# Routing, experts and combination of a top-2 mixture-of-experts layer in one block: two threshold bits a step, tokens gathered by slot, expert weights kept, last norm by tile

## The reference, cut to what matters

```
logits = xf @ router_w.T ; probs = softmax(logits)        # 2048 tokens, 8 experts
topw, topi = top_k(probs, 2) ; topw = topw / (topw.sum + 1e-6)
order = lexsort((-fw, fe))                                 # by expert, then by falling weight
rank = arange(N * K) - starts[se] ; keep = rank < capacity # capacity = 320
disp[e, slot] = xf[token]                                  # 8 x 320 rows of 128
eo = (silu(disp @ wg) * (disp @ wu)) @ wd                  # 128 -> 512 -> 128, by expert
out[token] += eo[expert, slot] * weight * keep
x = layernorm(x + out)
```

## Time and profile before

| | us |
|---|---|
| three timed runs | 2526.57, 2539.88, 2541.69 |
| median | 2539.88 |
| the profiled execution's own time | 2530.64 |
| its span, first to last instruction | 2528.8 |

### The profile page before, as it was taken

One profiled execution on the slowest core, in us unless ns is written; L12 is line 12 of the kernel. 1 busy time (PEld: TensorE's weight loads), 2 busy tenths in 40 slices (PEclk: granted clock), 3 DMA queues, 4 the chain that ended last, 5 costly groups with the idle time before them and its releaser, 6 DMA issues. The chain is left out here.

```text
span 2528.8 us, 55963 instructions
## 1 busy us (share of the span) xinstructions
PE 2023.5 (80%) x20339; PEld 1352.8 (53%) x20339; DVE 1867.9 (74%) x3645; ACT 1636.9 (65%) x3008; POOL 1248.1 (49%) x1115
## 2 busy tenths in 40 slices
PE   4388888279999999999999999999999998311370
PEld 2133332236776767777677767777677766210250
DVE  5566661389999999999999999999999993354013
ACT  2045556158888888888888888888888886100120
POOL 0100000177777677777777766777777762001415
PEclk8589998689999999999999999999999999555695
DMA  2412300311111120112101110112101110000222
GB/s 84 82 15 27 40 2 2 110 41 35 32 30 35 35 78 28 35 35 79 35 27 35 59 55 27 35 35 79 35 27 35 35 35 18 23 26 6 75 94 50
DMA packets 69952, 105.66 MB, mean 42 GB/s; under 512 B 21942, under 2 KB 44092, under 8 KB 69020
## 3 DMA queue, kind: packets, MB, share of 16 engines
q1 hardware_dynamic: 66996, 96.61, 14.1%
q0 software_dynamic: 2688, 5.51, 0.8%
HBM read 41.73 MB, written 10.42 MB: 21 GB/s over the span
## 5 line engine op out<-in xcount | busy, mean ns | idle before, releaser
L755 PE MATMUL pA<-layer_weights,x_feature_major 128*128 128x512 f32 x768 | 400.1, 603 | 32.4 <-DMA window_mask<-in_mask_dram 16.4
L1328 POOL TENSOR_TENSOR qk<-rot_cos,rot_sin 128x512 f32<-128x512 f32 x256 | 323.6, 1275 | 156.0 <-DVE rot_sin L1129 156.0
L1127 DVE TENSOR_TENSOR rot_cos<-pA,layer_tab 128x512 f32<-128x512 f32 x384 | 262.8, 684 | 76.7 <-ACT sq L968 70.3
L399 ACT ACTIVATE probs_by_key<-pT 128x512 f32<-128x512 f32 (+3 forms) x384 | 176.5, 489 | 206.9 <-PE pT L352 173.1
L1338 POOL TENSOR_TENSOR qk<-qk,rnorm 128x512 f32<-128x512 f32 x256 | 263.5, 1045 | 88.6 <-DVE rnorm L1162 88.6
L968 ACT ACTIVATE sq<-pA 128x512 f32<-128x512 f32 x384 | 228.5, 595 | 67.5 <-PE pA L755 58.0
L417 DVE TENSOR_REDUCE minus_max<-pS 128x1 f32<-128x1024 f32 (+7 forms) x256 | 184.2, 753 | 110.3 <-PE pS L326 110.0
L1139 DVE TENSOR_REDUCE sumsq<-sq 128x8 f32<-128x512 f32 x384 | 253.4, 671 | 14.6 <-ACT sq L968 14.4
L1129 DVE TENSOR_TENSOR rot_sin<-pA,layer_tab 128x512 f32<-128x512 f32 x384 | 260.8, 679 | 0.0
L1028 ACT ACTIVATE probsT<-pD 64x512 f32<-64x512 f32 x384 | 226.3, 589 | 43.7 <-PE pD L796 40.2
L1345 POOL TENSOR_TENSOR probs<-probs,row_inverse 128x1024 f32<-128x1024 f32 x96 | 182.7, 1903 | 101.6 <-DVE row_inverse L1198 101.6
(11 more groups left out here) (285 smaller groups left out, 4374.6 us busy)
## 6 DMA issues: line engine op xcount, KB each, us to landing
v_shifted<-v SPq DMA_DIRECT2D x96, 384.0 KB, 3.5
v_shifted<-v SPq DMA_DIRECT2D x95, 128.0 KB, 3.4
layer_weights<-in_Wqkv_dram SPq DMA_DIRECT2D x24, 384.0 KB
q_stack<-stacked SPq DMA_DIRECT2D x72, 64.0 KB
k_stack<-stacked SPq DMA_DIRECT2D x72, 64.0 KB
stacked<-part SPq DMA_DIRECT2D x24, 128.0 KB, 1.9
layer_weights<-in_Wo_dram SPq DMA_DIRECT2D x6, 512.0 KB
w_gate<-in_wg_dram SPq DMA_DIRECT2D x8, 256.0 KB, 2.7
```

Source lines behind the costliest of these rows:

```text
L755: pe.matmul(A[c % 2][:, :], cols(X0f, s), slot(s, QKV_AT + 512 * c, 512), start=True, stop=True).then_inc(q_ready[c], 1)
L1127: dve.tensor_tensor(t1[c % 2][:, :].rearrange("p (h g d) -> p h g d", g=2, d=32), a, tabl[s % 2][:, j].unsqueeze(1).broadcast_to([P, 8, 2, ...
L1328: pool.tensor_tensor(qk(s, c), t1[c % 2][:, :], t2[c % 2][:, :], ALU.add).then_inc(added[c], 1)
```

## The change

Lines with + are new and lines with - are removed. `route`, `experts`, `combine`, the last `layernorm_all` and `store_tokens` become one block, `routed_experts`. The tokens (x_stored) and all weights of all experts are sent from SP at its start.

The parts that change:

- The key is turned on TensorE, so that its 128 (tile, expert) pairs lie on the partitions and the 128 tokens of a tile on the free axis. The threshold takes 15 unrolled steps of two bits, three candidates each; the compare also writes its own count.
- Slots are counted along the free axis by a scan. The value goes back through TensorE to token order, and a product of two one-hot matrices (32 matmuls) gives the token of each slot (`idx`).
- GpSimd gathers the 20 slot tiles from DRAM into SBUF. No row is scattered or zeroed.
- Each gathered tile is turned once. TensorE's order is up(e, 0), down(e-1), up(e, 1 to 3), turn(e+1). Results are stored from SP, one buffer per expert.
- The norm's statistics are taken by tile behind the sums, the power by batches of 4, 4, 4, 2 and 2 tiles on GpSimd between its gathers, and the result is stored by batch.

```diff
+    TURNS = [(-(-e * CAP // P), -(-(e + 1) * CAP // P)) for e in range(EX)]
+    LN_BATCHES = [(0, 4), (4, 8), (8, 12), (12, 14), (14, 16)]
...
         @block.sync
+            sp.dma_start(w["tokens_in"].rearrange("(t p) d -> p t d", p=P), X[:, :, :]).then_inc(x_stored, 16)
+            for e in range(EX):
+                sp.dma_start(WG[:, e, :], w["wg"][e]).then_inc(w_loaded[e], 16)
+                sp.dma_start(WU[:, e, :], w["wu"][e]).then_inc(w_loaded[e], 16)
+                sp.dma_start(WD[:, e, :, :], w["wd"][e].rearrange("(c p) n -> p c n", p=P)).then_inc(w_loaded[e], 16)
+            for e in range(EX):
+                at = e * CAP
+                sp.wait_ge(y_kept, e + 1)
+                sp.dma_start(w["expert_out"][at:at + CAP - PARTIAL, :].rearrange("(c p) d -> p c d", p=P), yo[e][:, 0:CT - 1, :])\
+                    .then_inc(y_stored, 16)
+                sp.dma_start(w["expert_out"][at + CAP - PARTIAL:at + CAP, :], yo[e][0:PARTIAL, CT - 1, :]).then_inc(y_stored, 16)
+            out = w["result"].rearrange("(t p) d -> p t d", p=P)
+            for t0, t1 in LN_BATCHES:
+                sp.wait_ge(normed, t1)
+                sp.dma_start(out[:, t0:t1, :], X[:, t0:t1, :]).then_inc(stored, 16)
+            sp.wait_ge(stored, 16 * len(LN_BATCHES))
 
...
         @block.tensor
+            pe.wait_ge(key_done, 1)
+            pe.transpose(bank[0][:, 0:P], key[:, :, :].rearrange("p t e -> p (t e)"), ident[:, :]).then_inc(key_turned, 1)
+            for i in range(BIT_STEPS):
+                pe.wait_ge(compared, 3 * i + 3)
+                pe.matmul(bank[6][:, 0:3], cst[:, SUM_AT:SUM_AT + P], cnt[:, :], start=True, stop=True).then_inc(counted, 1)
+            pe.wait_ge(tile_counted, 2)
+            pe.matmul(bank[7][:, 0:2], cst[:, AHEAD_AT:AHEAD_AT + P], ncol[:, :], start=True, stop=True)
+            pe.matmul(bank[7][:, 2:3], cst[:, SUM_AT:SUM_AT + P], ncol[:, 0:1], start=True, stop=True).then_inc(offset_ready, 1)
+            pe.wait_ge(val_done, 2)
+            for k in range(2):
+                mm = pe.matmul(bank[0][:, 0:P], val[:, k, :], ident[:, :], start=(k == 0), stop=(k == 1))
+            mm.then_inc(val_ready, 1)
+            pe.wait_ge(eq_done, 2)
+            pe.wait_ge(ids_p, 1)
+            for c in range(PICKS):
+                if c % 8 == 0:
+                    pe.wait_ge(hot_done, c // 8 + 1)
+                mm = pe.matmul(bank[1][:, 0:2 * SLOT_TILES], hotL[:, c, :], hotR[:, c, :, :], start=(c == 0), stop=(c == PICKS - 1))
...
+            def turn(e):
+                t0, t1 = TURNS[e]
+                pe.wait_ge(slots_in[e], 16 * (t1 - t0))
+                if e >= 2:
+                    pe.wait_ge(xt_kept, e - 1)
+                for t in range(t0, t1):
+                    mm = pe.transpose(XT[e % 2][:, (t - t0) * P:(t - t0 + 1) * P], xg[:, t, :], ident[:, :])
+                mm.then_inc(xt_ready, 1)
...
+            turn(0)
+            for e in range(EX):
+                up(e, 0)
+                if e >= 1:
+                    down(e - 1)
+                for f in range(1, FC):
+                    up(e, f)
+                if e + 1 < EX:
+                    turn(e + 1)
+            down(EX - 1)
...
         @block.gpsimd
+            pool.wait_ge(x_stored, 16)
+            pool.wait_ge(idx_done, 1)
+            for e in range(EX):
+                for t in range(*TURNS[e]):
+                    pool.indirect_dma_start(out=xg[:, t, :], out_offset=None, in_=w["tokens_in"],
+                                            in_offset=bass.IndirectOffsetOnAxis(ap=idx[:, t:t + 1], axis=0)).then_inc(slots_in[e], 16)
+            pool.wait_ge(half_set, 1)
+            pool.wait_ge(gat_done, 1)
+            pool.wait_ge(y_stored, 32 * EX)
+
+            def root(b):
+                t0, t1 = LN_BATCHES[b]
+                pool.wait_ge(eps_done, b + 1)
+                pool.tensor_tensor(rstd[:, t0:t1], ve[:, t0:t1], half[:, t0:t1], ALU.pow).then_inc(rooted, 1)
+            due = {6: 0, 10: 1, 14: 2}
+            for t in range(TILES):
+                for k in range(TOPK):
+                    c = k * TILES + t
+                    pool.indirect_dma_start(out=got[:, t, k, :], out_offset=None, in_=w["expert_out"],
+                                            in_offset=bass.IndirectOffsetOnAxis(ap=gat[:, c:c + 1], axis=0)).then_inc(arrived[t], 16)
+                if t in due:
+                    root(due[t])
+            root(3)
+            root(4)
...
         @block.vector
+            dve.wait_ge(key_turned, 1)
+            link(dve.tensor_copy(keyT[:, :], bank[0][:, 0:P]))
+            for i in range(BIT_STEPS):
+                T, nxt = acc[i % 2], acc[(i + 1) % 2]
+                dve.tensor_tensor(cand[:, :].bitcast(I32), bits[:, i, :], T[:, 0:1].bitcast(I32).broadcast_to([P, 3]), ALU.bitwise_or)\
+                    .then_inc(cand_done, 1)
+                dve.wait_ge(cand_done, i + 1)
+                for j in range(3):
+                    dve.tensor_scalar(junk[:, j, :], keyT[:, :], cand[:, j:j + 1], None, ALU.is_ge, ALU.add, accum_out=cnt[:, j:j + 1])\
+                        .then_inc(compared, 1)
+                dve.wait_ge(counted, i + 1)
+                dve.scalar_tensor_tensor(T[:, 1:4], bank[6][:, 0:3], float(CAP), cand[:, :], ALU.is_ge, ALU.mult).then_inc(took, 1)
+                dve.wait_ge(took, i + 1)
+                dve.tensor_reduce(nxt[:, 0:1], T[:, 0:4], AX.X, ALU.max).then_inc(T_done, 1)
+                dve.wait_ge(T_done, i + 1)
...
+            for k, op in enumerate((ALU.is_gt, ALU.is_equal)):
+                dve.tensor_scalar(over[:, k, :], keyT[:, :], T, None, op, ALU.add, accum_out=ncol[:, k:k + 1]).then_inc(tile_counted, 1)
+            dve.wait_ge(tile_counted, 2)
+            for k in range(2):
+                dve.tensor_tensor_scan(along[:, k, :], unit[:, 0:1].broadcast_to([P, P]), over[:, k, :], 0.0, ALU.mult, ALU.add).then_inc(chain, 1)
+            n[0] += 2
...
+            for c in range(0, PICKS, 8):
+                dve.tensor_tensor(hotL[:, c:c + 8, :], rows1[:, :].unsqueeze(1).broadcast_to([P, 8, P]),
+                                  low1[:, c:c + 8].unsqueeze(2).broadcast_to([P, 8, P]), ALU.is_equal).then_inc(hot_done, 1)
+                if c == 0:
+                    dve.wait_ge(eq_done, 1)
+                    dve.tensor_tensor(hotR[:, :, 1, :], eqH[:, :, :],
+                                      cst[:, TILE_AT:TILE_AT + PICKS].unsqueeze(2).broadcast_to([P, PICKS, SLOT_TILES]), ALU.mult)\
+                        .then_inc(eq_done, 1)
+            dve.wait_ge(idx_ready, 1)
+            link(dve.tensor_copy(idh[:, :], bank[1][:, SLOT_TILES:2 * SLOT_TILES]))
+            dve.scalar_tensor_tensor(idx[:, :], idh[:, :], float(P), bank[1][:, 0:SLOT_TILES], ALU.mult, ALU.add).then_inc(idx_done, 1)
...
+            for b, (t0, t1) in enumerate(LN_BATCHES):
+                for t in range(t0, t1):
+                    dve.wait_ge(arrived[t], 32)
+                    for k in range(TOPK):
+                        c = k * TILES + t
+                        dve.scalar_tensor_tensor(Z[:, t, :], got[:, t, k, :], keepw[:, c:c + 1],
+                                                 (X if k == 0 else Z)[:, t, :], ALU.mult, ALU.add).then_inc(y_sum, 1)
+                        dve.wait_ge(y_sum, 2 * t + k + 1)
+                    dve.bn_stats(st[:, t, :], Z[:, t, :]).then_inc(stats, 1)
+                    dve.wait_ge(stats, 2 * t + 1)
+                    dve.bn_aggr(mv[:, t, :], st[:, t, :]).then_inc(stats, 1)
+                dve.wait_ge(stats, 2 * t1)
+                dve.tensor_scalar(ve[:, t0:t1], mv[:, t0:t1, 1], EPS, None, ALU.add).then_inc(eps_done, 1)
+                dve.wait_ge(rooted, b + 1)
+                for t in range(t0, t1):
+                    dve.tensor_scalar(X[:, t, :], Z[:, t, :], mv[:, t, 0:1], rstd[:, t:t + 1], ALU.subtract, ALU.mult).then_inc(normed, 1)
```

More of the change, by code:

```diff
@@ L1539, in sem @@
             return ctx.enter_context(nc.semaphore(name))
[L1541 to L1542 removed]
+        U32 = mybir.dt.uint32
         rw = sb("router_rows", [EX, D])
@@ L1545, in route @@
         xT = sb("xT_route", [P, TILES, P])
-        cst = sb("route_tab", [P, 4, ET])
-        bits = sb("bit_tab", [P, BITS], I32)
-        tri = sb("tri_ones", [P, 2, P], BF16)
-        zero = sb("zero_rows", [P, SLOTS // P, D])
-        Lg, Pr, Pq, oh1, oh2, key, tmp, tmp2, keep, slot = (et(n) for n in (
-            "logits", "probs", "probs_rest", "first", "second", "key", "tmp", "tmp2", "keep", "slot"))
-        flagb = sb("flags", [P, EX, TILES], BF16)
-        flag2 = sb("flags_kept", [P, EX, TILES], BF16)
@@ L1554, in route @@
-        cum = sb("cumulated", [P, ET])
-        m = sb("token_max", [P, 10, TILES])
-        T = sb("threshold", [P, EX])
-        cand = sb("candidate", [P, EX])
-        cnt = sb("count", [P, 2, EX])
-        acc = sb("accepted", [P, EX])
-        bank = [ctx.enter_context(nc.psum_tensor(f"pQ{r}", [P, 512], F32)) for r in range(8)]
```

(49 more changed lines are left out.)

428 lines of the change are left out of this document (141 added, 287 removed).

## The result

| | before | after |
|---|---|---|
| median of four runs (us) | 2539.7 | 2454.62 |
| lowest and highest | 2526.57, 2541.69 | 2432.58, 2461.72 |
| the profiled execution's span | 2528.8 | 2459.9 |
| end of the third norm, from where the code differs | 2233.49 | 2256.91 |
| from there to the end (the tail) | 295.31 | 202.99 |

The changed kernel takes 0.9623 of the time before, 95% interval 0.9583 to 0.9663. In a later comparison it was 0.9627 (0.9578 to 0.9677). The two medians of the table divide to 0.9665, just outside that interval, and the record doesn't say how the 0.9623 is worked out: by whole times the size of the gain is open by about 0.4% of the time.

The account below looks back on a forecast made before the run. The prediction took the last 295 us for a chain of latencies with engines mostly idle. Its terms sum to -89.7 us: 2441 from the profiled execution, 2450 from the median; it took 2447, with 2426 to 2473 holding over 8 in 10.

Parts of the forecast that it names:

- key: Router key: fewer DVE operations and reductions over neighbouring values, against a new TensorE turn and copy; -0.3 us, bounds -1 and +1.
- threshold: Threshold search: 15 unrolled steps of 2.3 us for 30 looped of 2.1; 34.7 us against 63.0, -28.3 us.
- slots: Slot numbering by scans, one-hot operations and matmuls: 14.0 us against 12.8, +1.2 us, bounds -2 and +5.
- hand-over: Routing to TensorE's first turn: three gathers and a landing, 6.0 us, replace 49.7 us with 32 scatters; -43.7 us.
- experts: Experts' rounds: 8.6 us against 9.65, without load wait but with a 0.6 us copy wait; -6.3 us, bounds -9 and -2.
- combination, norm, store: Last stages: 32 gathers with powers between, norm by tile, smaller last store; 57.3 us against 69.6, -12.3 us, bounds -16 and -3.
- Rival 1: Threshold: a step costs 3.3 us, all upper bounds at once; time 2462, with slots at their bound 2466; chance 0.10.
- rival 3: Hand-over: gathers don't run ahead of the experts, each waiting for all 20; +21 us, time 2468; chance 0.03.
- Rival 4: Experts: TensorE's clock stays low throughout, up to 60 us more; time 2500; chance 0.02.
- rival 5: Experts held up by weights sharing DMA engines with gathers, late below 100 GB/s; the slower case, time 2570; chance 0.02.
- Rival 2: Last norm: GpSimd pays for each change between powers and gathers, 23 us for three powers; time 2470; chance 0.06.
- Rival 6: Whole change: steps or experts are serial in some other way and half the gain is gone; time 2492; chance 0.03.

Follow-up runs that it names:

- Experiment 7: Changed kernel, but TensorE waits for all 20 token gathers before its first turn: hand-over 27.59 us, 21.5 more; experts' stage 74.07 us.
- experiment 10: Changed kernel run again unaltered: median 2445.42 us of six runs, ratio 0.9627 to the kernel before, tail 202.01 us.
- Experiment 5: Changed kernel with weights of experts 2 to 7 sent only behind the stores of the second expert before each: experts' stage 103.55 us, 29.1 more.
- experiment 2: Changed kernel with 30 unrolled threshold steps of one bit and one compare instead of 15 of two bits: threshold 48.33 us, 1.61 a step.
- experiment 9: Changed kernel with the last norm and store as before, over all 16 tiles behind the combination: first gather to end 65.2 us, tail 11.7 us longer.
- experiment 4: Changed kernel with the next expert's rows turned and copied early instead of last in the round: experts' stage 69.93 us, 4.5 less; tail 199.00 us.
- experiment 11: Changed kernel with bf16 flag sum, early turn of expert rows and all last-norm roots behind the last gather: 2434.06 us, 0.9573 of the kernel before.
- Experiment 1: Kernel before with only its 30-step threshold loop unrolled on DVE and TensorE: threshold 47.99 us where it had taken 63.07, tail 284.17 us.

## Why the prediction was right, step by step

The tail was forecast to lose 89.7 us and lost 92.3; the ratio puts the time at 2539.7 x 0.9623 = 2444, and the median was 2454.62, where 2447 was said. What the mechanism forecast is the tail. That the whole time came within 8 us is partly luck: the four runs of the changed kernel lie 29 us apart, and 2447 was a choice between two bases.

| step | predicted | measured |
|---|---|---|
| key | -0.3 | -0.5 |
| threshold | -28.3 | -30.8 |
| slots | +1.2 | +0.7 |
| hand-over | -43.7 | -44.5 |
| experts | -6.3 | -4.3 |
| combination, norm, store | -12.3 | -12.8 |

*Threshold.* The step is 2.15 us and not 2.3. The compares cost 0.88 where 1.08 was taken, since each starts 0.27 us behind the one before although it lasts 0.35; the sum and the wait for it cost 0.69 where 0.60 was taken, the small operations 0.59 for 0.63. The Trainium skill (VectorE: DVE Perf Modes, section "Two Vector instructions with no wait between them") has an operation with an accumulator output as two instructions. The trace agrees: a read of 83 ns stands behind each of the 45 compares. But it costs no 0.2 us: it starts with the next compare, and only the third read, 0.08 us, stands in the chain. Rival 1 fell with that.

*Slots.* 13.4 us where 14.0 was forecast. The one-hot rows took 1.2 us, as forecast from their width. The group in the changed kernel:

```profile
L1869 DVE TENSOR_TENSOR slot_row_hot<-row_numbers,slot_row 128x1024 bf16<-128x1024 bf16 x4 | 4.7, 1220 | 0.0
```

That is 1.2 ns a column, in bf16 from SBUF. The Trainium skill's tier table (VectorE: DVE Perf Modes, section "The perf-mode tier table (the rule you actually need)"), of which the prediction said that it would make the sum 2 us lower, isn't borne out for these operands. The Trainium skill (the same page, section "What auto-detection actually checks") has the engine double its rate if every tensor is 16-bit with step 1 or -1; the slot's row number is one value held over 128 columns. The trace agrees with that condition, though no run here varied the step.

*Hand-over.* The forecast of 6.0 us counts from GpSimd's first gather; from there it took 2328.72 - 2323.49 = 5.2, and 6.1 with the 0.9 us of lag ahead of it, which the kernel before had too. The forecast added three whole gathers and a landing, but the third starts only 2.75 us behind the first, and the turn follows 2.48 us later. Experiment 7 shows that 21.5 of the 44.5 us hang on TensorE waiting for three gathers only: rival 3 would have given back 21 us, and that is what it does when it is built. The rest, the scatters and the reload that are gone, is read from the rows; no run puts them back.

*Experts.* The round is 8.67 us against 8.6. The stage fell short by 2.0 us, and 1.4 of them are the clock in its first expert. The stretches of the first expert and of the next six in the changed kernel:

```profile
2328.72:2338.62 9.90, 8.74 (x21) 5.50 (x21) 1.75 (x4) 2.52 (x6) 7.55 (x8) 0.61 0.18 53
2338.62:2390.64 52.02, 48.53 (x256) 35.52 (x256) 11.71 (x25) 15.01 (x42) 7.54 (x8) 1.00 0.10 31
```

The first ran at 0.61 of the clock, mostly the low level of 1.2 GHz. From the first turn to the second 8.94 us passed, where it had been 7.55 in the kernel before and was 7.58 in experiment 10. There the stage took 73.05 us, 5.7 less than before, so 1.4 of the 2.0 us are of this execution only. The other 0.6 are a miscount: the prediction saved seven rounds less 1 us for the drain, 6.3 in all, but six rounds lie between the second turn and the last, which gave 6.1, and what follows the last turn took 0.4 us longer (13.47 for 13.07). Rival 4 (low clock throughout) and rival 5 (weights late) fell: the clock is 1.00 and no wait for weights appears. The 7 MB had landed before the threshold was found, having moved at 287 GB/s in the key's stage, three times the rate at which rival 5 decides. Experiment 5 shows what it costs when TensorE does wait for weights, though there because they are sent late and not, as in rival 5, because transfers share the engines.

*Combination, norm and store.* A root between gathers costs GpSimd this much (timeline of the changed kernel):

```profile
2422.45 0.94 POOL L1768 DMA_INDIRECT gathered<-expert_out,gathers  x1 [0.30 <-issue]
2423.42 1.04 POOL L1763 TENSOR_TENSOR norm_rstd<-norm_var_eps,root_exponent 128x4 f32<-128x4 f32 x1
2424.66 1.08 POOL L1768 DMA_INDIRECT gathered<-expert_out,gathers  x1 [0.20 <-issue]
2426.04 1.04 POOL L1768 DMA_INDIRECT gathered<-expert_out,gathers  x1 [0.30 <-issue]
2427.39 0.94 POOL L1768 DMA_INDIRECT gathered<-expert_out,gathers  x1 [0.30 <-issue]
```

From gather to gather across it pass 2.21 us for 1.25, and the next two are 0.1 us slower each: 1.2 us a root, 1.3 forecast. Rival 2 fell; the load of about 6 us of which the Trainium skill tells (GPSIMD Engine Reference, section "Instruction dispatch") appears at none of these three changes there and back. The first gather came 3.0 us behind the last copy (3.3 forecast), the last normalisation 49.9 us behind the first gather (51), and the last store took 3.9 us (3). Rival 6 is out with the stages' own gains, and experiments 2, 7 and 9 each undo one part and lose what that part was said to bring.

So no step failed; the experts' is the furthest off in proportion. The largest error of a term is 2.5 us, in the threshold, and it came mostly from adding the compares' durations instead of their start-to-start distance. The errors partly cancel: threshold and hand-over brought more than forecast, the experts less.

## What to carry to other kernels

A tail in which no engine is busy is priced by its hand-overs, and these can be forecast from the timeline (here the sum to 3%, each stage to 2.5 us); take the distance from start to start, not the duration, wherever independent operations follow each other on one engine. When a kernel's runs spread by more than the effect, measure from the event where the code begins to differ. A load's place is judged by its lead over its first use: with 1.3 us of lead six experts' weights cost 29 us here, some 9 us of it slower products at a clock that fell in the pauses, and a round earlier they cost nothing.

## What the runs showed of the hardware

**The clock of a front part that never changed.** All kernels have the same code up to the third norm, whose end lay anywhere from 2229.90 to 2257.22 us in the thirteen profiled executions. The granted clock from 100 to 600 us goes with it. This stretch in experiment 4 and in experiment 11, the earliest and the latest end (the number before the last two is the clock):

```profile
100.00:600.00 500.00, 384.52 (x2815) 171.85 (x2816) 295.89 (x485) 251.42 (x523) 80.05 (x74) 0.87 0.18 38
```

```profile
100.00:600.00 500.00, 389.75 (x2496) 165.20 (x2494) 274.29 (x444) 231.65 (x486) 60.33 (x57) 0.80 0.18 36
```

The third norm ended at 2229.90 and at 2257.22. TensorE was busy for about the same time in both, but at the lower clock it got through fewer products: 2496 for 2815. The others lie between (0.87 with 2233.49 in the kernel before, 0.81 with 2256.91 in the changed kernel; then 0.87 with 2230.88 to 2235.57, 0.86 with 2233.33 and 2239.19, 0.85 with 2242.64, 0.84 with 2241.37 and 2244.66, 0.83 with 2248.95). From 600 to 2200 us the clock is 0.98 or 0.99 in all thirteen. The changed kernel itself was at 0.86 and 2239.19 when it ran again, so it isn't the kernel. That the clock makes the difference is read from thirteen executions that agree; no run sets it. What decides which execution keeps the high level in the first 600 us stays open.

**One stretch at either level.** Experiment 1 showed the same 32 passes at 0.96 and at 0.50 of the clock: 3.75 and 6.83 us.

**The price of f32 on three columns.** Two passes, 0.59 us together at the low level, against 0.18 for one in bf16.

**The turn of a hardware loop**, with the operand that it indexes and TensorE looping beside, cost DVE 14.8 us of standing at 29 turns, 0.51 each, and unrolling both loops gave back 15.1.
